# Attention scheduling: the second side task of a pair of steps is moved from behind the products with V to directly behind the first side task, into another PSUM bank

## The reference, cut to what matters

```python
def _L0_attn_b_ref(x, w_kv_down, w_kv_up, w_q, w_out):     # x: 2 x 2048 x 256
    latent_kv = x @ w_kv_down                              # rank 128
    kv = latent_kv @ w_kv_up
    k, v = kv[..., :HD], kv[..., HD:]                      # 16 heads of 64
    q = (x @ w_q).reshape(Bx, Tx, N_HEAD, HEAD_SIZE)
    att = jnp.einsum('bqhd,bkhd->bhqk', q, k) * HEAD_SIZE ** -0.5
    att = jnp.where(causal, att, -jnp.inf)
    att = jax.nn.softmax(att, axis=-1)
    y = jnp.einsum('bhqk,bkhd->bqhd', att, v).reshape(Bx, Tx, HD)
    return y @ w_out

x = x + ssm(layernorm(x));  x = x + mixer(layernorm(x))
x = x + attention(layernorm(x));  x = x + mixer(layernorm(x))
```

## Time and profile before

| | |
|---|---|
| median of 3 runs | 2234.52 us (2222.45 to 2241.63) |
| the profiled execution, its own time | 2223.86 us |
| its span in the trace | 2222.5 us |
| TensorE's granted clock, mean over the span | 0.978 of 2.4 GHz |
| TensorE busy (matmuls) | 2044.9 us, 92% |
| GpSimd, VectorE, ScalarE busy | 64%, 60%, 50% |
| TensorE in the steps of attention, 299 to 2125 us | 1725.5 us busy of 1826 |

### The profile page before, as it was taken

The page is one execution under the profiler, slowest core; times in us unless marked ns, Lnnn a source line. Parts: engine busy times, 40 slices in busy tenths (PEclk is TensorE's granted clock), DMA queues, the critical chain, the costliest instruction groups (busy, mean ns, idle before and its releaser), DMA issues.

```text
span 2222.5 us, 35662 instructions
## 1 busy us (share of the span) xinstructions
PE 2044.9 (92%) x13104; PEld 1262.4 (57%) x13104; DVE 1329.0 (60%) x2711; ACT 1101.2 (50%) x2226; POOL 1426.6 (64%) x812
## 2 busy tenths in 40 slices
PE   5998679999999999999989999999999999999999
PEld 3666445655555555565555555555555555555466
DVE  5888556566656565656555656575656565646353
ACT  4775534444444444444454444444444444444575
POOL 1333216777777777777756677867777777777822
PEclk9999689999999999999999999999999999999999
DMA  3000000000000000000000000000000000000001
GB/s 111 1 1 0 8 8 10 6 23 6 23 6 23 6 23 6 23 6 23 6 18 10 18 11 18 11 18 10 18 11 18 11 18 11 18 10 11 25 25 57
DMA packets 25787, 37.03 MB, mean 17 GB/s; under 512 B 6544, under 2 KB 14864, under 8 KB 25616
## 3 DMA queue, kind: packets, MB, share of 16 engines
q1 hardware_dynamic: 25616, 34.76, 5.0%
HBM read 30.02 MB, written 4.46 MB: 16 GB/s over the span
## 4 chain that ended last, share of the span: by engine, by line
PE 68%; DVE 19%; ACT 6%; issue 5%; POOL 2%; DMA 0%; ACTq 0%; DVEq 0%; POOLq 0%
PE heads_out L826 19%; PE beside L645 15%; PE two_heads L783 8%; PE scores L806 4%; PE scores L812 4%; PE scores L810 4%; PE scores L808 4%; DVE part_max L1014 4%; PE scores L645 2%; DVE stats L865 2%; ACT prob L1227 2%; PE beside L837 2%; PE beside L791 2%; DVE X L1058 2%; DVE wP_lo L979 1%
## 5 line engine op out<-in xcount | busy, mean ns | idle before, releaser
L1312 POOL TENSOR_TENSOR acc<-acc,prob 128x1024 f32<-128x1024 f32 (+3 forms) x512 | 1017.2, 1987 | 218.5 <-ACT prob L1227 162.6
L1227 ACT ACTIVATE prob<-scores 128x512 f32<-128x512 f32 (+3 forms) x1280 | 579.4, 539 | 630.6 <-DVE scores L1024 327.3
L1014 DVE TENSOR_REDUCE part_max<-two_heads 128x2 f32<-128x1024 f32 x384 | 468.5, 1220 | 301.6 <-PE two_heads L783 301.3
L826 PE MATMUL heads_out<-prob,V 128*64 128x512 f32 (+3 forms) x2560 | 546.7, 549 | 0.0
L783 PE MATMUL two_heads<-k_hi,q_hi 64*128 64x512 f32 (+3 forms) x1280 | 277.6, 429 | 73.0 <-DVE part_max L1011 40.3
L1011 DVE CUSTOM_DVE_ANT_0 two_heads<-two_heads,mask 128x128 f32<-128x128 f32 (+3 forms) x512 | 241.5, 513 | 128.1 <-PE two_heads L783 128.0
L826 PEld LDWEIGHTS heads_out<-prob,V 128*64 128x64 f32 x2560 | 157.2, 137 | 229.8 <-issue 208.8
L783 PEld LDWEIGHTS two_heads<-k_hi,q_hi 64*128 64x128 f32 x1280 | 120.7, 184 | 240.4 <-issue 100.2
L806 PE MATMUL scores<-q_hi,k_hi 64*128 64x512 f32 (+3 forms) x1280 | 236.2, 364 | 1.1 <-ACT neg_max L1214 0.8
L810 PE MATMUL scores<-q_lo,k_hi 64*128 64x512 f32 (+3 forms) x1280 | 235.5, 362 | 0.0
L812 PE MATMUL scores<-neg_max,sel 64*128 64x512 f32 (+3 forms) x1280 | 235.4, 362 | 0.0
(11 more groups left out here) (291 smaller groups left out, 2989.5 us busy)
## 6 DMA issues: line engine op xcount, KB each, us to landing
rden<-rden_rows SPq DMA_DIRECT2D x128, 128.0 KB, 2.9
wP_raw<-wPair SPq DMA_DIRECT2D x16, 384.0 KB, 3.1
X<-u SPq DMA_DIRECT2D x8, 512.0 KB, 8.7
out<-X SPq DMA_DIRECT2D x8, 512.0 KB, 2.9
den<-den_rows SPq DMA_DIRECT2D x64, 4.0 KB
rden_rows<-inverse SPq DMA_DIRECT2D x64, 4.0 KB, 1.3
wA_sb<-wA SPq DMA_DIRECT2D x1, 768.0 KB, 6.8
wFa<-wF SPq DMA_DIRECT2D x1, 768.0 KB, 7.8
```

What stands on the lines that cost most here:

```text
L826: made = pe.matmul(heads_out[head(h), x0:], V[(idx - j + c) % NVS][:, tt, head(h)], prob[step % NPROB][:, h, x0:], start=t == 0, stop=t == ...
L1014: made = ve.reduce_max(part_max[:, t, :, c:c + 1], two_heads[:, :, 0:width], AX.X)
L1227: ac.activation(prob[step % NPROB][:, h, x0:], bank(task, h)[:, x0:], ACT.Exp).then_inc(empty(task, h)[0], 1)
L1312: po.tensor_tensor(total[:, :, x0:], total[:, :, x0:], new[:, :, x0:], ALU.add).then_inc(acc_ok, 1)
```

## The change: what it does

In a pair of steps that has no diagonal step, `filler(s + 8)` is now called directly behind the first side task, with the bank of side tasks set to 0 instead of 7; behind the products with V it is called only in diagonal pairs. It is now called in a pair in which the denominators are due, too. Bank 0 is the first bank of the scores: it holds head 0's scores of the even step of the same pair, and is written again by the even step of the next pair.

```diff
+        self.side_bank = 7
...
         if self.in_steps:
-            return (7,)
+            return (self.side_bank,)
...
             filler(10 ** 6)
+            diagonal = not steps[s:s + 2] or any(t >= TPB * UNITS[idx][2] for idx, t in steps[s:s + 2])
+            if not diagonal:
+                self.side_bank = 0
+                filler(s + 8)
+                self.side_bank = 7
             while self.at < goal - 1:
                 maximum()
...
-            if not due("denominators"):
+            if not due("denominators") and diagonal:
                 filler(s + 8)
```

## The result

The changed kernel takes 2167.51 us (median of 4 runs, 2165.39 to 2168.69), the kernel before, in the same comparison, 2235.18 us (4 runs, 2222.45 to 2241.63). The ratio is 0.970, with a 95% interval of 0.966 to 0.975: faster by 67.7 us, where 35 were forecast. The profiled executions are 55.2 us apart (2223.86 and 2168.69).

The account below looks back on a forecast made before the run. TensorE, busy 92% of the span with 68% of the chain, and its waits on VectorE were taken as the bound. Savings of 10.5 + 14.6 + 10.4 = 35.5 us, taken as 35, took the 2234.5 us median to 2199.5; range 2185 to 2229.

Parts of the forecast that it names:

- Part 1: First pairs of a unit with both projection halves: less waiting for bank 7, 0.35 us at 30 places, 10.5 us saved.
- it waits some 0.15 us with the semaphore: Next scores in first pairs of a unit: TensorE waits some 0.15 us until VectorE has emptied bank 0.
- Part 2: The other 73 second side tasks: one change of matmul shape less, 0.2 us each, 14.6 us saved.
- Part 3: 13 diagonal pairs lose the key projection in front; second maximum starts 0.8 us sooner each, 10.4 us saved.
- by the same 35 us the median goes to 2199.5: Whole kernel: the saving read from a 2223.9 us profiled execution is taken unchanged from the 2234.5 us median.
- A: Rival for second side tasks: changes of shape cost nothing, only 16 us saved, median 2218; chance 0.14.
- B: Rival at the next scores: bank 0 becomes a slower wait; at 0.7 us a place, median 2271; chance 0.08.
- C: Rival for diagonal pairs: something else holds the second maximum, 25 us saved, median 2209; chance 0.13.
- D: Rival for the whole path: won time returns as waits for GpSimd, median 2230 to 2238; chance 0.10.
- I am wrong if it grows to tens: Sign against the forecast: the exponentials' wait for GpSimd grows beyond 12 us to tens.

Follow-up runs that it names:

- Run 1: Kernel before with only the second side task's bank changed from 7 to 2 in pairs without a diagonal step: 2227.89 us, ratio 0.997.
- run 3: Changed kernel with the second side task between the two products with V of the pair, still in bank 0: 2224.51 us, ratio 0.995.
- run 10: Kernel before with the second task directly behind the first, in bank 0, only in the first diagonal pair of units with j = 2: 2210.59 us, ratio 0.990.
- run 9: Kernel before, unchanged, run again for a second trace: 2237.71 us.
- run 5: Changed kernel plus VectorE reductions of 512 and 256 constant columns before one maximum's reduction in the last pair of units with j = 2: 2210.84 us, ratio 0.990.
- run 6: Changed kernel plus three VectorE reductions of 512 constant columns before one maximum's reduction in the last pair of units with j = 2: 2236.47 us, ratio 1.001.
- run 4: Changed kernel without the second side task in pairs where denominators are due, as in the kernel before: 2208.82 us, ratio 0.988.
- run 7: The kernel of run 4, with diagonal pairs also getting their second task directly behind the first, in bank 0: 2185.03 us, ratio 0.978.
- run 8: Changed kernel with diagonal pairs treated alike, their second task directly behind the first in bank 0: 2172.84 us, ratio 0.973.
- run 11: Changed kernel with the second side task in bank 2, the first bank of the odd step, instead of bank 0: 2172.07 us, ratio 0.972.
- run 12: Changed kernel with a unit's first diagonal pair treated like the pairs without a diagonal: 2169.46 us, ratio 0.971.
- run 2: Changed kernel with the second side task left in bank 7 at its new place: 2324.39 us, ratio 1.040.

## Why the prediction was right in kind and wrong in size

**Part 1, 30 first pairs at 0.35 us: right in mechanism, the wait in it was not there.** The pairs 6 and 12 win 0.47 and 0.49 us, the whole of what the sum had before its last step. The step that failed is "it waits some 0.15 us with the semaphore". I had put the second addition 0.68 behind the first, and VectorE starts it 0.60 behind; it ends 2.86 us behind the first maximum (617.04 to 619.90), not 2.96. The weights of the scores are loaded 0.16 behind the maximum instead of 0.11, but the first matmul of the scores comes no later behind it than before, and the saving from maximum to maximum stays. 30 x 0.48 = 14.4 instead of 10.5 us. Run 1 splits it: 0.28 to 0.30 go with the free bank, the other 0.2 with the place.

**Part 2, 73 second tasks at 0.2 us: right, and a little small.** Pair 15 wins 0.20 with one second task. Pairs 7 to 10 win 0.94 with three, 0.3 each. The back-to-back half takes 0.80 here, 1.0 when it stands apart, and a second task set apart costs its pair 0.35 for two changes of shape (run 3). The Trainium skill (TensorE: Matmul & The Clock Gate, section "The mechanism") lets a weight load overlap a running matmul only if the row groups differ. The trace after disagrees at the place shown: the load for the second half starts at 618.07, together with the last matmul of the first half, and both use 128 rows. By the rule, as the prediction had read it, this part would have been zero.

**Part 3, 13 diagonal pairs at 0.8 us: the wait was right, its price was not, and this is the step that put the forecast out of its range.** Pair 11 wins 0.85 us, and 0.84 with the key alone (run 10). But the 14 tasks moved there (13 keys and a query) are worth 27 us of the median, not 11. I priced TensorE's idle by its length, and the sum has no term for the clock. What the idle also did was to let the clock fall, in 2 of 15 places of the trace that I had, in 8 of 15 of an ordinary execution; and "by the same 35 us the median goes to 2199.5" took over a trace that lies 0.5% below the median as though the difference had nothing to do with the change. It had: run 9 shows that the difference is these falls, runs 5 and 6 that the wait brings them, and the kernel after, which has none there, is also without the spread (3.3 us over its runs, before 19). That step costs the forecast 11.3 us; with the 1.2 by which after's median lies below its profiled execution it makes 12.5. The range could not hold it either: its lower end, 2185, takes the same median (and is 49.5 us below it, not 48).

**What is left.** Of the 32 us by which the forecast was off, 12.5 are between traces and medians. Another 4 are the first part, 4 the two falls in the profiled execution. 7.4 stand in the pairs of heads 1 and 10, where VectorE also makes statistics of a layer norm; I had taken them for ordinary. The key is the smaller part of it: with the key alone (run 10) these two win 1.1 or 1.2 us where an ordinary pair of heads wins 0.7, but without the moved key (run 4) number 10, which has no fall there, takes 109.7 us and wins 5.0, an ordinary one 1.9. So of the 3.7 us that each wins beyond an ordinary one some 3 go with the place of the other second tasks. 1.3 of them are in pair 16, where TensorE's wait for a plain reduction goes from 1.56 us to 0.31 (number 1); why, no run tells. The other 4 are what is won in 6, 14, 7, the last and by part 2, less what the first loses. In 6 and 14 it goes with the dropped condition on denominators: run 7, which keeps it and has the key moved, takes 1.4 us more in each. In 7 each of the two traces has a fall of its own. The first pair of heads, which loses 5.2 us, is open; every run that moves the second task in all pairs without a diagonal lost there, runs 3, 4, 7, 8, 11 and 12 among them, and runs 1 and 10 did not. One more fall in the trace after (at its pair 5, 8.02 us against 6.41 in run 11) is 1.6 of it.

**The rivals.** A (shapes cost nothing) is refuted by run 3 and by the back-to-back rows. B (bank 0 becomes the wait) isn't there with the whole of the products with V as cover; run 2 shows its size in the old bank (1.4 us a place), run 3 with half of the cover (0.14 to 0.31 us). C (diagonal pairs don't move) is refuted by 1.68 us. D: the wait of ScalarE for GpSimd did grow to 53.1 us, yet the chain has GpSimd at 3%. "I am wrong if it grows to tens" was a bad sign to name: it looks at a wait on an engine that has time to spare, and should have asked for TensorE's wait for that engine.

## What to carry to other kernels

Two side tasks in a row, each with a bank of its own, beat two side tasks apart, as long as enough stands between the second one and the next user of its bank: here 0.8 us of products with V and a maximum were enough for a half, 1.9 us for a key. Take the bank away and it is 4% slower than before. Before an idle of TensorE is priced by its length, look at the granted clock in stretches of 10 us behind it, in more than one trace: here 1.2 us of idle behind narrow matmuls cost another 1.6 or 3.2 us in 8 of its 15 places in one execution, in 2 in another. A kernel whose runs spread by 1% on one core, and whose profiled run lies at the fast end, may be showing just that, and then the median is not the trace plus a constant.

## What the runs showed of the hardware

**The clock can fall behind a short wait.** TensorE waited 1.2 us (1.7 in two of the pairs of heads) behind scores of 256 and 128 columns, and the granted clock fell from 2.4 to 1.2 GHz shortly behind that in 2 and in 8 of 15 places of two executions of one program, in 13 of 15 with 1.28 us behind the same scores and other side tasks ahead (run 5), and in all 15 with 2.1 us (run 6). With 0.36 us of idle at the same place it fell in none (after; number 7 still has 1.22 there, and no fall). The first pair of heads, which has another wait of 0.7 to 0.9 us in its pair 11, does have a fall there in runs 7, 8, 10, 11 and 12. It costs a pair of heads 1.6 us, or 3.2 where it lasts twice as long, seen as 0.83 and 0.66 to 0.68 in stretches of 10 us. The Trainium skill (TensorE: Matmul & The Clock Gate, section "A second HAM failure mode: psum-queue depth-cycling") tells of short idles between groups of matmuls, frequent enough, that make the clock go up and down. These rows agree in kind, but here one such place in a pair of heads of 110 us was enough.

**The length of the wait alone doesn't tell.** In run 2 TensorE waits 41 times for 1.4 to 1.6 us behind matmuls of 512 columns in the 13 pairs of heads counted there, and the clock falls 3 times. Behind the narrow scores 1.28 us were enough in 13 of 15 places. The wait and what ran ahead of it were not varied one by one, so what of the matmuls ahead matters stays open.

**A run can move the falls without moving any order of its own near them.** Run 1 differs from the kernel before only in a bank, and has a fall behind 9 of its 15 pairs 11, with the clock at 0.969 over the span; its runs spread from 2221 to 2241 us as before's do. What decides between two executions whether a place falls isn't worked out here.
